# Graph layer on one core: six places for pairs of one-hots instead of four, and the next span's table word loaded inside the loop over pairs

## The chip, the core and the metric

The kernel runs on one NeuronCore of a Trainium2 chip. The metric is the device time of one execution in microseconds (us). TensorE is called PE here and its queue of weight loads PEld, VectorE is DVE, ScalarE is ACT, GpSimd is POOL and SyncE is SP. Each engine has a sequencer that reads the instructions in order, does register work, loads of registers from memory, waits and branches by itself, and hands the rest to its engine.

## What is computed

For 6250 nodes with 256 features and 200,000 edges, sorted by destination (fewer edges the higher the node, since the destinations are drawn as 6250 times a square):

```
agg   = segment_sum(x[src], dst, 6250)
h     = relu(agg @ W_rel + b_rel + x @ W_root)
i, f, g, o = split(h @ W_ih.T + b_ih + b_hh, 4)
h2    = sigmoid(o) * tanh(sigmoid(i) * tanh(g))
out   = layernorm(x + h2 @ W_fc + b_fc)
```

## The kernel before

The nodes lie in 25 groups of 250. The edges lie in chunks of 128, and four chunks are a step (or, in the dense part, a pair of one-hots, which also covers four chunks). The sum over edges is done in two ways.

**Gathered tiles.** For the last 21 groups, as 42 tiles of 125 nodes, POOL gathers the rows of x by the edges' source numbers: per step it copies four columns of source numbers into `idx` (L370) and issues four indirect DMAs (L400) into a ring of seven steps (`rows`). DVE makes a one-hot of the destinations for each step (L906), and PE multiplies it with the gathered rows into `ps_agg` (L476). SP reports each gathered step (L339), and PE's first matmul of a later step gives the ring's slot back to POOL (`steps_summed`, L396). The first seven steps gather from x itself (L385) before the main loop.

**Dense groups.** For the first four groups, where the edges are many, the adjacency is built as a matrix of counts. A window is ten nodes and holds two spans of five nodes; a group has 25 windows and 50 spans. For each span a packed word in `table` (written by DVE in the setup, L856) says which chunks it covers. PE and DVE each walk the same windows, spans and pairs: `unpack` (L297) loads the word into a register (L299) and splits it into first and past (L300), and a loop whose length is known only at run time goes over the span's pairs. In it DVE (`span`, L884) waits for a free place (`pairs_summed`, L891), makes `rel` (L892), `hot_lo` (L894) and `hot_key` (L897), and PE (`windows`, L436) waits for `pairs_ready` (L449), multiplies the four chunks of the pair (L451), and reports the place free. `next_pair` (L305) counts in registers. There are four places (`PAIRS`). Each window begins with a matmul that zeroes its bank (L441) and ends with a marker (L434), after which ACT copies it into `adj` (L639). After a group's 25 windows, `adj` is multiplied with x (L464) in seven batches, loaded into the memory of the pairs' places.

**Order.** Each engine walks a list of turns. A turn has four parts. In a part, PE does half of a tile's steps (`part_sum`, which begins with a load of its own from the table, L484), then a quarter of the gate matmuls of the group before (L537), then the part's windows: three each in the turns of the first dense group (four in its last part), two, two, three and two in those of the other three dense groups, whose last turn has seven windows for the four parts. The windows of one part are called a burst here. After the fourth part come the first layer (L519, L524) and the last (L545). DVE does the same order: one-hots of the part, then the pairs of its burst, then the pieces of the cell and the norm. So there are 8 bursts in the first dense group, around 105 to 362 us, and 12 in each of the others, around 602 to 796, 1000 to 1174 and 1365 to 1540 us.

**Setup.** DVE works out the tables from the destinations, splits x into a high and a low half piece by piece (written to `x_parts`), and reduces the source numbers to what `hot_lo` and `key` need (L858 to L866). POOL starts its first step when the table of tiles is there (L361) and the edges are in (L362).

Of the kernel before, what the change touches and what calls it, by code (L numbers as in the profile page):

```python
# [34 lines left out]
PAIRS = 4  # L35
# [22 lines left out]
T_COLS = T_SPAN + SPANS  # L58
# [67 lines left out]
def gnn_kernel(nc, x, xT, xb, srcT, dstT, dstq, w_rel, w_root, w_ihT, w_fc, b_rel, b_ih, b_hh, b_fc, out):  # L126
# [7 lines left out]
    with ExitStack() as ctx:  # L134
        def sb(name, shape, dt=f32):
            return ctx.enter_context(nc.sbuf_tensor(name, shape, dt))
# [14 lines left out]
        src_sb = sb("src_sb", [P, CHUNK_COLS], i32)  # L151
# [41 lines left out]
        dst_next = flat[0:QP, QPC * CHUNK:(QPC + 1) * CHUNK].bitcast(i32)  # L193
        cell_flat = cell[:, :, :].rearrange("p i n -> p (i n)")
# [47 lines left out]
        edges_in = sem("edges_in")  # L242
        bias_in = sem("bias_in")
# [53 lines left out]
        def unpack(engine, regs, at):  # L297
            packed, first, past = regs
            engine.reg_load(packed, table[0:1, at:at + 1] if isinstance(at, int) else table[0:1, ds(at, 1)])  # L299
            engine.reg_alu(first, packed, PACK, ALU.python_divide)  # L300
            engine.reg_alu(past, first, -PACK, ALU.mult)
            engine.reg_add(past, past, packed)
            return engine.snap(first, min_val=0, max_val=CHUNKS - 1), engine.snap(past, min_val=1, max_val=CHUNKS)
# [9 lines left out]
        @block.sync  # L313
        def _(sp):
            sp.dma_start(dstq_sb, dstq[0:QP * QPC * CHUNK].rearrange("(p c e) -> p c e", p=QP, c=QPC)).then_inc(dstq_in, 16)
            sp.dma_start(dst_next, dstq[QPC * CHUNK:(QP + 1) * QPC * CHUNK].rearrange("(p e) -> p e", p=QP)[:, 0:CHUNK]).then_inc(dstq_in, 16)
            sp.dma_start(src_sb[:, :], srcT).then_inc(edges_in, 16)
            sp.dma_start(dst_i, dstT).then_inc(edges_in, 16)
            sp.sem_inc(gathered, RING)
            for i in SP_PIECES:  # L320
                wait_split(sp, i)
                sp.dma_start(piece_target(i), piece(i)).then_inc(piece_out[i % PARTS], 16)
            for i in range(PARTS + 1):
                sp.wait_ge(piece_out[i], 16 * max(len(range(i, X_WHOLE, PARTS)), 1))
            sp.dma_start(wroot_sb[:, :, :], w_root.rearrange("(k p) n -> p k n", p=P)).then_inc(weights_in, 16)
            sp.dma_start(wrel_sb[:, :, :], w_rel.rearrange("(k p) n -> p k n", p=P)).then_inc(weights_in, 16)
            wih_v = w_ihT.rearrange("(k p) n -> p k n", p=P)
            sp.dma_start(wih_sb[:, :, 0:D_H], wih_v[:, :, 0:D_H]).then_inc(weights_in, 16)
            sp.dma_start(wih_sb[:, :, D_H:3 * D_H], wih_v[:, :, 2 * D_H:4 * D_H]).then_inc(weights_in, 16)
            sp.dma_start(wfc_sb[:, :, :], w_fc.rearrange("(k p) n -> p k n", p=P)).then_inc(weights_in, 16)  # L330

            sp.wait_ge(table_ready, 1)
            steps = sp.value_load(table[0:1, T_STEPS:T_STEPS + 1], min_val=2 * TILES, max_val=MAX_STEPS)
            sp.wait_ge(gathered, 2 * RING)
            with sp.Fori(1, (steps + (RING - 1)) // RING) as r:
                for k in range(RING):
                    for j in range(QC):
                        sp.wait_ge(landed[k][j], r * 16 + 16)
                    sp.sem_inc(gathered, 1)  # L339

        @block.gpsimd
        def _(pool):
# [19 lines left out]
            pool.wait_ge(edges_in, 32)  # L362
# [6 lines left out]
            def copy_index(chunk, k, j):  # L369
                g.tensor_copy(idx[:, k % RING, j:j + 1], src_sb[:, ds(chunk + j, 1)]).then_inc(idx_copied, 1)  # L370
# [5 lines left out]
            for k in range(RING):  # L376
# [6 lines left out]
                pool.sem_inc(steps_begun, 1)  # L383
                for j in range(QC):
# [24 lines left out]
        def _(pe):  # L409
# [18 lines left out]
            pe.reg_mov(place, 0)  # L428
            pe.reg_mov(step_0, 0)
# [6 lines left out]
            def windows(w0, n_windows):  # L436
                for i in range(n_windows):
# [4 lines left out]
                    for side in range(2):  # L442
                        at = w * 2 + (T_SPAN + side)
                        o = bank[:, side * SCOLS:(side + 1) * SCOLS]
                        first, past = unpack(pe, pe_regs, at)
                        with pe.Fori(first, past, QC):
# [5 lines left out]
                            last.then_inc(pairs_summed, 1)  # L452
                            next_pair(pe, pair_0, place, more_places)
# [284 lines left out]
        def _(dve):  # L738
# [101 lines left out]
            dve.sem_inc(table_ready, 1)  # L840
            split_pieces(POOL_PIECES, PARTS)
# [16 lines left out]
            dve.wait_ge(edges_in, 32)  # L858
            v.tensor_copy(dst_u[:, :], dst_i).then_inc(setup, 1)
            v.tensor_scalar(src_part, src_sb[:, :], P - 1, None, ALU.bitwise_and).then_inc(setup, 1)  # L860
            v.tensor_scalar(src_high, src_sb[:, :], P.bit_length() - 1, None, ALU.logical_shift_right).then_inc(setup, 1)
            n_setup[0] += 3
            dve.wait_ge(setup, n_setup[0])
            link(v.tensor_copy(src_lo[:, :], src_part))
# [11 lines left out]
            dve.reg_mov(place, 0)  # L876
            step_0 = dve.alloc_register("step_0")
# [6 lines left out]
            def span(w, side):  # L884
                at = w * 2 + side
                static = isinstance(w, int)
                first, past = unpack(dve, dve_regs, at + T_SPAN)
                with dve.Fori(first, past, QC) as c:
# [6 lines left out]
                                    src_lo[:, ds(c, QC)].rearrange("p (q c) -> p q c", c=2).unsqueeze(2).to_broadcast([P, PQ, P, 2]), ALU.is_equal)  # L895
                    dve.wait_ge(rel_made, s + 1)
# [187 lines left out]
```

## Time and profile before

| | |
|---|---|
| runs of the kernel before | 1822.73, 1830.2, 1832.34 us (median 1830.2) |
| profiled execution, own time | 1824.41 us |
| its span, first to last instruction | 1822.5 us |
| mean granted PE clock | 0.91 of full speed |

The page gives the busy time of each engine and its share of the span; register work, loads into registers, branches and waits are not counted as busy. In the chain of work that ended last, and among the waits, "issue" is time in which the engine waited for nothing that the profile shows, and PEldq, DVEq or POOLq mark the sequencer's own steps, which only the views by line list.

### The profile page before, as it was taken

How to read it: one execution, taken by the hardware profiler on the slowest of the kernel's cores; microseconds unless marked ns; L12 is line 12 of the kernel's file. 1: busy time of each engine (PE TensorE's matmuls, PEld its weight loads, DVE VectorE, ACT ScalarE, POOL GpSimd, SP SyncE). 2: the span in 40 equal slices, each digit the busy share in tenths (PEclk: the TensorE clock that was granted, in tenths of full speed). 3: DMA queues.
4: the chain of work that ended last, by engine and by line, in shares of the span. 5: the costliest groups of instructions: out<-in, count | busy, mean ns of one | idle time of the engine just before them, and what ended most of it. 6: DMA issues, size and time to landing. Idle time of an engine off the chain costs nothing.

```text
span 1822.5 us, 31499 instructions
## 1 busy us (share of the span) xinstructions
PE 1513.5 (83%) x6882; PEld 1213.0 (67%) x6883; DVE 815.9 (45%) x1763; ACT 418.5 (23%) x743; POOL 1281.0 (70%) x1926
## 2 busy tenths in 40 slices
PE   0157688697988898788998889899988888999997
PEld 0023355486767676667887667688876676888886
DVE  8877666431322654531324565422244654222332
ACT  0001021110112332220222333212223332222333
POOL 5875877777777877877777668776763668656640
PEclk9976677698988998889999999999998998999999
DMA  9563555576766555567766445576652455766540
GB/s 342 209 233 87 150 161 145 157 225 207 215 195 180 162 162 165 161 198 223 223 206 180 138 133 166 160 246 217 203 155 77 133 146 161 225 189 177 150 122 18
DMA packets 131966, 319.14 MB, mean 175 GB/s; under 512 B 17295, under 2 KB 68268, under 8 KB 130198
## 3 DMA queue, kind: packets, MB, share of 16 engines
q0 software_dynamic: 75264, 245.95, 46.4%
q10 hardware_dynamic: 52632, 54.80, 9.5%
q1 hardware_dynamic: 3936, 16.62, 2.4%
q8 instruction: 82, 1.34, 0.3%
q14 instruction: 52, 0.43, 0.1%
HBM read 298.10 MB, written 19.20 MB: 174 GB/s over the span
## 4 chain that ended last, share of the span: by engine, by line
PE 48%; POOL 21%; issue 19%; DVE 4%; DMA 3%; DVEq 3%; POOLq 1%; ACT 0%; ACTq 0%; SPq 0%
PE ps_blk L537 20%; POOL rows L400 14%; PE ps_agg L476 9%; PE ps_win L464 6%; POOL idx L370 6%; PE ps_y L545 4%; PE ps_blk L519 3%; PE ps_blk L524 3%; PE ps_tr L451 1%; DMA hot_key<-in_xb 1%; POOL rows L385 1%; PE ps_win L451 1%; DMA rows<-x_parts,idx 1%; POOLq L370 1%; DMA wih_sb<-in_x 1%
## 5 line engine op out<-in xcount | busy, mean ns | idle before, releaser
L400 POOL DMA_INDIRECT rows<-x_parts,idx x924 | 963.5, 1043 | 453.5 <-PE ps_agg L476 157.6
L537 PE MATMUL ps_blk<-cell,wih_sb 128*128 128x250 f32 x2400 | 545.5, 385 | 2.9 <-issue 2.2
L537 PEld LDWEIGHTS ps_blk<-cell,wih_sb 128*128 128x128 f32 x2400 | 464.1, 196 | 69.5 <-issue 8.8
L476 PE MATMUL ps_agg<-rows,onehot 128*125 x1112 | 341.8, 462 | 153.2 <-SPq L339 70.8
L476 PEld LDWEIGHTS ps_agg<-rows,onehot 128*125 128x125 f32 x1112 | 234.1, 216 | 227.5 <-issue 175.9
L906 DVE SCALAR_TENSOR_TENSOR onehot<-iota_f,tile_first,dst_u 128x500 f32 (+1 forms) x278 | 207.0, 746 | 291.7 <-PE ps_agg L476 171.6
L370 POOL COPY idx<-src_sb 128x1 int32 x956 | 264.4, 277 | 16.7 <-issue 9.7
L664 ACT ACTIVATE cell<-ps_blk,bg_sb 128x250 f32<-128x250 f32 x300 | 140.8, 470 | 544.0 <-PE ps_blk L537 470.2
L897 DVE TENSOR_TENSOR hot_key<-iota_h,rel 128x980 f16 x263 | 174.4, 663 | 0.4 <-issue 0.4
L464 PE MATMUL ps_win<-adj,hot_key 128*128 128x250 f32 x784 | 170.7, 375 | 2.4 <-DMA hot_key<-in_xb 1.5
L464 PEld LDWEIGHTS ps_win<-adj,hot_key 128*128 128x128 f32 x784 | 148.0, 190 | 21.6 <-DMA hot_key<-in_xb 4.0
L892 DVE TENSOR_SCALAR rel<-key,span_key x263 | 66.7, 254 | 186.0 <-issue 116.8
L451 PE MATMUL ps_win<-hot_key,hot_lo 128*128 x640 | 113.1, 315 | 34.4 <-issue 20.2
L894 DVE TENSOR_TENSOR hot_lo<-iota_h,src_lo 128x512 f16 x263 | 141.5, 538 | 0.3 <-issue 0.3
L451 PE MATMUL ps_tr<-hot_key,hot_lo 128*128 x412 | 83.2, 312 | 51.3 <-issue 36.3
L451 PEld LDWEIGHTS ps_win<-hot_key,hot_lo 128*128 x640 | 63.7, 100 | 78.2 <-issue 57.5
L519 PE MATMUL ps_blk<-x_t,w_sb 128*128 128x250 f32 x400 | 105.0, 398 | 0.6
L932 DVE TENSOR_TENSOR cell<-cell 128x250 f32<-128x250 f32 x100 | 42.1, 421 | 129.1 <-ACT cell L664 98.1
L451 PEld LDWEIGHTS ps_tr<-hot_key,hot_lo 128*128 x412 | 40.7, 99 | 89.0 <-issue 70.6
L937 DVE TENSOR_TENSOR cell<-cell 128x250 f32<-128x250 f32 x100 | 40.0, 420 | 124.5 <-ACT cell L657 102.8
L524 PE MATMUL ps_blk<-cell,w_sb 128*128 128x250 f32 x400 | 94.6, 378 | 0.0
L639 ACT ACTIVATE adj<-ps_win 128x490 f32<-128x490 f32 x58 | 59.7, 1029 | 146.8 <-PE ps_win L434 90.5
(125 smaller groups left out, 914.2 us busy)
## 6 DMA issues: line engine op xcount, KB each, us to landing
hot_key<-in_xb ACTq DMA_DIRECT2D x28, 896.0 KB
rows<-x_parts,idx POOLq DMA_INDIRECT x924
x_t<-in_xT ACTq DMA_DIRECT2D x25, 250.0 KB
x_n<-in_x ACTq DMA_DIRECT2D x25, 250.0 KB
out<-y ACTq DMA_DIRECT2D x25, 250.0 KB
x_parts<-wih_sb SPq DMA_DIRECT2D x4, 1024.0 KB, 6.8
wih_sb<-in_x ACTq DMA_DIRECT2D x6, 512.0 KB, 9.7
x_parts<-cell SPq DMA_DIRECT2D x2, 1024.0 KB, 7.6
```

The source lines that it names most:

```text
L370: g.tensor_copy(idx[:, k % RING, j:j + 1], src_sb[:, ds(chunk + j, 1)]).then_inc(idx_copied, 1)
L400: g.indirect_dma_start(rows_f[:, k * QC + j, :], None, x_parts, bass.IndirectOffsetOnAxis(ap=idx[:, k, j:j + 1], axis=0)).then_inc(landed[ ...
L451: last = mm(o, hot_lo[:, ds(half, 1), j // 2, :, j % 2].squeeze(1), hot_key[:, ds(half, 1), j // 2, :, j % 2].squeeze(1), start=False, sto ...
L464: last = mm(ps_win[:, c * GN:(c + 1) * GN], xs[:, b, c * P:(c + 1) * P], adj[:, i * X_BATCH + b, :], start=(i == 0 and b == 0 and c == 0), ...
L476: ins = mm(o, onehot[:, hot * QC + j, 0:TN], rows[:, ds(slot + j, 1), :].squeeze(1), start=(first and j == 0), stop=False)
L519: mm(ps_blk[m % BANKS][:, 0:GN], wroot_sb[:, k, m * P:(m + 1) * P], x_t[:, k, :], start=(k == 0), stop=False)
L524: last = mm(ps_blk[m % BANKS][:, 0:GN], wrel_sb[:, k, m * P:(m + 1) * P], agg_t[:, k, :], start=False, stop=(k == KI - 1))
L537: last = mm(o, wih_sb[:, k, col:col + P], h_t[:, k, :], start=(k == 0), stop=(k == KH - 1))
L664: nc.scalar.activation(dst[:, j, :], ps_blk[b % BANKS][:, 0:GN], fn, bias=bg_sb[:, bias + j:bias + j + 1]).then_inc(gate_done, 1)
L894: v.tensor_tensor(hot_lo[:, ds(half, 1), :, :, :].squeeze(1), iota_h[:, 0:P, :].unsqueeze(1).to_broadcast([P, PQ, P, 2]), src_lo[:, ds(c, ...
L897: v.tensor_tensor(hot_key[:, ds(half, 1), :, :, :].squeeze(1), iota_h[:, :, :].unsqueeze(1).to_broadcast([P, PQ, SCOLS, 2]), rel[:, ds(hal ...
L906: v.scalar_tensor_tensor(onehot[:, ds(hot, QC), 0:TN], iota_f[:, 0:TN].unsqueeze(1).to_broadcast([P, QC, TN]), nodes, dst_u[:, ds(c, QC)]. ...
```

## The change

`PAIRS` goes from 4 to 6, so `rel`, `hot_lo` and `hot_key` have six places. The room comes from the source numbers: they stay in memory as 16-bit numbers (`src_u`), are brought in as 32-bit numbers into the last slot of the ring `rows` (`src_i`), and DVE copies them from there right after it has reported the table of tiles; POOL's first step waits for that copy, and its seventh waits until DVE has read the 32-bit numbers. POOL's copies into `idx` read 16-bit numbers. The load of a span's word leaves `unpack` and becomes `load_span`: one before the first window, and one in the body of each loop over pairs, for the span after; on PE it stands behind the four matmuls of the pair, on DVE between `hot_lo` and the wait before `hot_key`. Since it stands in the body, it is done once for each pair.

```diff
-PAIRS = 4
+PAIRS = 6
...
-T_COLS = T_SPAN + SPANS
+T_COLS = T_SPAN + SPANS + 1
...
-        src_sb = sb("src_sb", [P, CHUNK_COLS], i32)
+        src_u = sb("src_u", [P, CHUNK_COLS], u16)
...
+        src_i = flat[:, (RING - 1) * QC * D_ROW:(RING - 1) * QC * D_ROW + CHUNK_COLS].bitcast(i32)
...
+        src_short = sem("src_short")
+        src_read = sem("src_read")
...
-        def unpack(engine, regs, at):
+        def load_span(engine, regs, at):
+            engine.reg_load(regs[0], table[0:1, at:at + 1] if isinstance(at, int) else table[0:1, ds(at, 1)])
+
+        def unpack(engine, regs):
             packed, first, past = regs
-            engine.reg_load(packed, table[0:1, at:at + 1] if isinstance(at, int) else table[0:1, ds(at, 1)])
             engine.reg_alu(first, packed, PACK, ALU.python_divide)
...
-            sp.dma_start(src_sb[:, :], srcT).then_inc(edges_in, 16)
+            sp.dma_start(src_i, srcT).then_inc(edges_in, 16)
...
             pool.wait_ge(table_ready, 1)
-            pool.wait_ge(edges_in, 32)
+            pool.wait_ge(src_short, 1)
...
-                g.tensor_copy(idx[:, k % RING, j:j + 1], src_sb[:, ds(chunk + j, 1)]).then_inc(idx_copied, 1)
+                g.tensor_copy(idx[:, k % RING, j:j + 1], src_u[:, ds(chunk + j, 1)]).then_inc(idx_copied, 1)
...
                 pool.sem_inc(steps_begun, 1)
+                if k == RING - 1:
+                    pool.wait_ge(src_read, 2)
...
             pe.reg_mov(place, 0)
+            load_span(pe, pe_regs, T_SPAN)
...
-                        first, past = unpack(pe, pe_regs, at)
+                        first, past = unpack(pe, pe_regs)
                         with pe.Fori(first, past, QC):
...
                             last.then_inc(pairs_summed, 1)
+                            load_span(pe, pe_regs, at + 1)
                             next_pair(pe, pair_0, place, more_places)
...
             dve.sem_inc(table_ready, 1)
+            dve.wait_ge(edges_in, 32)
+            v.tensor_copy(src_u[:, :], src_i).then_inc(src_short, 1)
             split_pieces(POOL_PIECES, PARTS)
...
-            dve.wait_ge(edges_in, 32)
             v.tensor_copy(dst_u[:, :], dst_i).then_inc(setup, 1)
-            v.tensor_scalar(src_part, src_sb[:, :], P - 1, None, ALU.bitwise_and).then_inc(setup, 1)
-            v.tensor_scalar(src_high, src_sb[:, :], P.bit_length() - 1, None, ALU.logical_shift_right).then_inc(setup, 1)
-            n_setup[0] += 3
+            v.tensor_scalar(src_part, src_i, P - 1, None, ALU.bitwise_and).then_inc(src_read, 1)
+            v.tensor_scalar(src_high, src_i, P.bit_length() - 1, None, ALU.logical_shift_right).then_inc(src_read, 1)
+            n_setup[0] += 1
             dve.wait_ge(setup, n_setup[0])
+            dve.wait_ge(src_read, 2)
...
             dve.reg_mov(place, 0)
+            load_span(dve, dve_regs, T_SPAN)
...
-                first, past = unpack(dve, dve_regs, at + T_SPAN)
+                first, past = unpack(dve, dve_regs)
...
                                     src_lo[:, ds(c, QC)].rearrange("p (q c) -> p q c", c=2).unsqueeze(2).to_broadcast([P, PQ, P, 2]), ALU.is_equal)
+                    load_span(dve, dve_regs, at + (T_SPAN + 1))
                     dve.wait_ge(rel_made, s + 1)
```

## Rows read from the trace of the kernel before

**Rows 1.** The page: busy times of the engines, and the chain's shares.

```profile
PE 1513.5 (83%) x6882; PEld 1213.0 (67%) x6883; DVE 815.9 (45%) x1763; ACT 418.5 (23%) x743; POOL 1281.0 (70%) x1926
...
PE 48%; POOL 21%; issue 19%; DVE 4%; DMA 3%; DVEq 3%; POOLq 1%; ACT 0%; ACTq 0%; SPq 0%
```

**Rows 2.** Busy time by stretch, all engines, then granted clock and DMA.

```profile
105.00:152.50 47.50, 36.55 (x146) 17.93 (x145) 39.41 (x98) 3.07 (x3) 23.46 (x31) 0.62 0.36 109
152.50:865.00 712.50, 583.77 (x2564) 449.80 (x2563) 318.31 (x693) 146.33 (x248) 561.55 (x848) 0.85 0.61 178
865.00:1822.50 957.50, 884.52 (x4159) 741.14 (x4157) 374.87 (x864) 267.84 (x491) 621.79 (x960) 0.96 0.55 163
```

**Rows 3.** Waits of POOL in 100 to 600, 600 to 865, 865 on (total, times, longest).

```profile
POOL rows L400 <- PE ps_agg L476: 19.4, 1, 19.4
...
POOL rows L400 <- PE ps_agg L476: 6.0, 5, 3.0
...
POOL rows L400 <- PE ps_agg L476: 132.2, 18, 24.9
```

**Rows 4.** Waits of PE in 105 to 345, 152.5 to 865, and 865 on (two).

```profile
PE ps_agg L476 <- SPq L339: 18.7, 4, 5.8
...
PE ps_agg L476 <- SPq L339: 69.6, 18, 6.0
...
PE ps_agg L476 <- DVE onehot L906: 9.3, 4, 5.6
...
PE ps_agg L476 <- SPq L339: 1.2, 1, 1.2
```

**Rows 5.** Timeline of PE at the end of a late burst of four pairs.

```profile
1441.80 0.68 PE L451 MATMUL ps_tr<-hot_key,hot_lo 128*128 x4
1443.54 0.74 PE L451 MATMUL ps_tr<-hot_key,hot_lo 128*128 x4 [1.06 <-issue]
...
1445.64 1.67 PE L476 MATMUL ps_agg<-rows,onehot 128*125 x6 [1.10 <-issue]
```

**Rows 6.** PE's sequencer at L299, whole run (ns: shortest, median, longest).

```profile
L299 PEldq TENSOR_LOAD <-table x200: 296/302/323, 108.6 to 1537.9; - x100
L299 PEldq FUSED_REGOPS  x150: 51/53/79, 598.9 to 1537.8; - x150
```

**Rows 7.** The chain around the first span on DVE.

```profile
105.35 0.31 DVEq L299
...
105.69 0.23 DVEq L300
```

**Rows 8.** The chain inside the first burst.

```profile
134.41 0.20 issue
134.61 1.00 PE ps_tr L451 x4
135.61 0.69 issue
```

**Rows 9.** Pairs of the run; of the first burst; its span loads; L451 by stretch.

```profile
L897 DVE TENSOR_TENSOR hot_key<-iota_h,rel 128x980 f16 x263 | 174.4, 663 | 0.4 <-issue 0.4
...
L897 DVE TENSOR_TENSOR hot_key<-iota_h,rel x31: 655/662/670, 106.8 to 145.5; 128x980 f16 x31
...
L299 PEldq TENSOR_LOAD <-table x6: 297/309/322, 108.6 to 145.1; - x6
...
865.00:1300.00 435.00, 32.13 (x200) 19.44 (x200) 0.97 0.63 187
```

**Rows 10.** Timeline of DVE and of PE around one pair of the third burst.

```profile
189.19 0.66 DVE L897 TENSOR_TENSOR hot_key<-iota_h,rel 128x980 f16 x1
...
190.09 0.74 PE L451 MATMUL ps_win<-hot_key,hot_lo 128*128 x4 [0.51 <-DVE hot_key L897]
```

**Rows 11.** Groups by line: POOL's copy of source numbers; a 32-bit to 16-bit cast.

```profile
L370 POOL COPY idx<-src_sb x956: 192/193/1197, 32.0 to 1769.5; 128x1 int32 x192
...
L859 DVE CAST dst_u<-hot_key 128x1568 uint16<-128x1568 int32 x1 | 1.0, 976 | 0.2 <-DVE table L856 0.2
```

## The prediction

> **What bounds the kernel now.** The page says first that no engine is full: PE is busy 83% of the span and POOL 70%, and PE holds 48% of the chain, POOL 21% and "issue" 19% [rows 1]. Such shares are averages over stages, so I cut the span where the waits change their direction [rows 2].
>
> POOL's waits give the cuts [rows 3]. POOL waits once for PE, 19.4 us, until 152.4 us, while PE works through the first burst. From there to 865 us it waits 6.0 us in all, the longest 2.98 us at 657 us: it runs freely, and PE waits for gathered steps 18 times, 69.6 us [rows 4]. From 865 us on POOL waits 132.2 us for PE, and PE waits 1.2 us for steps. So PE sets the pace up to 152 us, POOL from 152 to 865 us, and PE after that. PE's time in the middle stretch is worth nothing except where it is late enough to hold POOL up.
>
> Inside the bursts, what limits PE? Not its array: the four matmuls of the last pair of a late burst begin 1.74 us after those of the pair before and take 0.74 us, with 1.06 us idle put down to issue [rows 5]. In the first burst an idle of 0.20 us stands between pairs of one span and one of 0.69 us where a span ends [rows 8]. This is PE's sequencer: branch, counters, load of the word, unpacking. And not DVE: in the tightest place that I found (third burst) the one-hot is done at 189.19 + 0.66 = 189.85 us and PE's matmul starts at 190.09 [rows 10]; in the late groups they are several us ahead. That idle is labelled with hot_key only because hot_key came last; what ended it was the sequencer. So DVE's places don't hold PE, although DVE waits for them.
>
> **The change, part by part.**
>
> *Two more places.* They remove waits of DVE for PE. PE doesn't wait for pairs, so nothing is gained there; what follows on DVE (next one-hots, cell products) comes earlier. From 865 us on PE's waits for one-hots of tiles are 9.3 us in four places, the longest 5.6 us [rows 4]; that one stands behind a group's product, where DVE waits for PE first, and the shorter ones are about as long as PE's own start of a part (1.10 us of issue, [rows 5]). I take 0; the bound is a gain of 9.3 us.
>
> *The load on PE.* A load takes 0.302 us on PE's sequencer, and the register work for a changing address 0.053 us [rows 6]. On DVE the load (0.31 us) and the next step stand 0.34 us apart [rows 7]. I take 0.35 us for a load on PE, and 0.45 us with the address work and its gap. The bounds are 0.05 us (the sequencer goes on while the load is under way, only its issue is paid) and 0.49 us (the whole extra idle of a span's end, 0.69 - 0.20, which holds the unpacking too, [rows 8]). Nothing covers it: it stands behind the pair's last matmul, when PE has nothing queued.
>
> Where the loop runs once for a span, the load only moves from behind the branch to ahead of it. Two things are added. The body's loads count pairs, not spans: 263 pairs [rows 9] for 200 spans, all 63 extra ones in the first dense group, since a late group has 200 / 4 = 50 pairs for its 50 spans [rows 9]. And the load for a burst's first span, which PE's sequencer did under the queued gate matmuls, now stands at the end of the burst before, with the load of `part_sum` or the first layer queued behind it.
>
> - First burst: 31 pairs, 6 loads before [rows 9]. Of the 31 loads after, 5 are those between spans; 26 are new on PE's path: 26 x 0.35 = 9.1 us. POOL waits for exactly this (19.4 us), so it starts its free stretch 9.1 us later. Bounds 1.3 and 12.7 us.
> - The seven other bursts of this group: 82 pairs for 44 spans, 38 + 7 = 45 loads, 15.8 us. PE waits 18.7 us for steps in 105 to 345 us [rows 4], which absorbs it almost; the last burst lies behind most of these waits, so I add 1.0 us. Bounds 0 and 3.
> - Second dense group: 12 bursts. Four of them lie ahead of POOL's wait at 657 us: 4 x 0.45 = 1.8 us. The other eight are absorbed by waits for steps. Bounds 0.4 and 2.4.
> - Last two dense groups, where PE sets the pace: 24 bursts x 0.45 = 10.8 us. Bounds 24 x 0.1 = 2.4 and 24 x 0.59 = 14.2.
>
> *The load on DVE.* It stands under `hot_lo` and takes 0.34 us [rows 7] of its sequencer, 25 more times in the first burst. There DVE's pairs follow one another at (145.5 - 106.8) / 30 = 1.29 us on the mean [rows 9], span ends included and partly held back by PE; with the loads that becomes at most 1.29 + 25 x 0.34 / 30 = 1.57 us. PE's mean pace becomes 1.20 + 5 x 0.49 / 30 + 25 x 0.35 / 30 = 1.57 us [rows 8] as well, so DVE barely stays off the path: 0, with an upper bound of 1 us.
>
> *Setup.* POOL's first step now waits for a cast of 128x1568 numbers on DVE; a cast of this size takes 0.976 us [rows 11]. POOL's first steps lie on the chain of waits. 1.0 us, bounds 0 and 1.5. The piece splits that DVE does next are 1.0 us later too. The seventh step's wait for `src_read` is for two operations that DVE does right after the table of spans, while POOL has six steps to issue first: 0.
>
> *16-bit source numbers on POOL.* 956 copies of 0.193 us [rows 11], in series with the indirect DMAs. The trace has no POOL copy that changes the type; DVE's cast of 1568 columns runs at the usual pace, and on POOL one column is all fixed cost. I take 0. In the stretch that POOL sets there are 848 / 2 = 424 copies [rows 2]; 0.05 us more on each (a quarter) would be 21 us, my upper bound. A cheaper copy would be worth at most the same the other way; I see no reason for one, as only 128 numbers are read either way.
>
> The sum is 1.0 + 9.1 + 1.0 + 1.8 + 10.8 = 23.7 us. The profiled execution took 1824.4 us, so it would take 1848.1. The median shown is 5.8 us above it and the three runs spread over 9.6 us, so a median may lie at 1848 to 1854; I forecast 1851.
>
> A rule bears on the load. The Trainium skill, Perfetto Trace Analysis, section on sequencer-only instructions, says that a sequencer reads its next instruction only after it has executed one and pushed its semaphore update. It speaks against this change: by it a load behind the matmuls is paid in full, as in my sum; were it wrong, the first rival below would hold. The trace agrees as far as it goes, with 0.34 us from a load of 0.31 us to the next step [rows 7], but there the next step needs the word.
>
> **Rivals.**
>
> 1. *Faster: the load runs beside what follows it.* Each load in the trace is followed by a step that needs its word, so its 0.30 us may be latency that `next_pair` and the branch would now cover. From the third pair of a late burst on, the loads are on the path: (50 - 24) x 2 = 52 spans x 0.30 = 15.6 us gained, against 24 x 0.1 at the bursts' ends, and -1.5 + 1.3 in the first burst, and the setup's 1.0: -12.4 + about 0 in the middle, so 1812 us by the profiled execution, 1815 as a median. It decides as soon as more than two thirds of a load are covered. Against it: every step of a sequencer in the chain follows the one before by its length and a small gap.
> 2. *The load costs, but less, and the sum stays in the noise.* At 0.10 to 0.15 us a load the terms shrink to about 3.5 + 1 + 5 us with the setup's 1.0 inside: +4 to +9 us, 1831 to 1836.
> 3. *The places pay some back.* If the 9.3 us of waits for one-hots [rows 4] were due to DVE's waits for places, the sum would be 14 us: 1842.
> 4. *POOL's copy costs more.* With 0.05 us on each, 21 us come on top: 1872.
> 5. *The change doesn't reach what it aims at* is my forecast in part: six places are filled, yet PE's pace in a burst doesn't move.
>
> **Chances.** About 9 us (0.5%) is what a measurement of this kernel can tell from no change. Forecast 0.62; rival 1 0.13; rival 2 0.11; rival 3 0.06; rival 4 0.08. So faster 0.13, same 0.12, slower 0.75. The likeliest case alone spans 1838 to 1864 (bounds of its terms, and the median's 6 us). The whole range leaves out rival 1 and the far ends: 1833 to 1876.
>
> **What would show it.** PE's steps in the first burst 1.55 us apart inside a span instead of 1.20, the burst about 9 us longer, and POOL's wait before 152 us grown to about 28 us. In a late burst the same 1.74 us between the last two pairs, and 1.10 us before the next part's first matmul grown to about 1.55. 263 loads on each sequencer. DVE's waits for places shorter, without effect. If instead the 1.74 us shrink to about 1.45, rival 1 holds; if POOL's copies are longer than 0.193 us, rival 4. What else would make it wrong: a granted PE clock in the late stretch that falls from its 0.96 [rows 2], because PE pauses more often between matmuls; 0.01 less over 884 us of busy time is up to 9 us.

## The result, and the profile after

The changed kernel takes 1838.65 us (median of 7 runs, 1836.6 to 1843.2); the kernel before 1830.2 (7 runs beside them, 1822.73 to 1832.34). The ratio is 1.0058, with a 95% interval of 1.0038 to 1.0078: a small loss (+8.45 us in the medians), of the sign that was predicted and about half its size or less (the forecast was +20.8 us). The profiled execution took 1836.6 us against 1824.4.

The page of the changed kernel: the engines' busy times, then the shares of the chain [rows 1].

```profile
PE 1508.9 (82%) x6882; PEld 1211.9 (66%) x6883; DVE 834.1 (45%) x1764; ACT 418.1 (23%) x743; POOL 1269.0 (69%) x1926
...
PE 49%; POOL 19%; issue 18%; DVEq 5%; DVE 5%; DMA 4%; POOLq 1%; ACT 0%; ACTq 0%; SPq 0%
```

PE and POOL do no more work. DVE is busy for 18 us more with operations of the same length (`hot_lo` 0.539 us in the mean against 0.538): its loads stand between them now, so they overlap less. The kernels with one engine's load below bear that out: with DVE's load alone DVE is busy for 832.0 us, with PE's alone for 815.2. DVE's waits for a free place got shorter, as forecast, and nothing came of it (before, then after: total, times, longest):

```profile
DVE rel L892 <- PE ps_win L451: 62.6, 19, 17.4
```

```profile
DVE rel L904 <- PE ps_win L459: 24.6, 19, 6.4
```

The three stretches of [rows 2], with their borders moved by what the first burst grew:

```profile
105.00:162.10 57.10, 37.41 (x147) 17.94 (x146) 42.38 (x98) 3.07 (x3) 22.28 (x31) 0.60 0.32 100
162.10:875.00 712.90, 580.86 (x2562) 446.99 (x2561) 326.21 (x693) 146.13 (x248) 561.43 (x851) 0.85 0.62 179
875.00:1834.70 959.70, 881.81 (x4160) 742.70 (x4158) 381.49 (x864) 267.59 (x491) 611.91 (x958) 0.96 0.56 162
```

The first stretch is 9.6 us longer for the same instructions, the middle one as long as before, the last one 2.2 us longer. POOL's waits for PE in 100 to 600, in 600 to 875 and from 875 us on (total, times, longest) answer to [rows 3], and PE's waits for gathered steps in 105 to 345 and in 152.5 to 865 us to [rows 4].

```profile
POOL rows L407 <- PE ps_agg L485: 30.6, 2, 30.5
...
POOL rows L407 <- PE ps_agg L485: 8.4, 5, 5.4
...
POOL rows L407 <- PE ps_agg L485: 147.1, 21, 25.4
```

```profile
PE ps_agg L485 <- SPq L344: 5.2, 1, 5.2
...
PE ps_agg L485 <- SPq L344: 52.3, 15, 7.0
```

POOL's first wait grew from 19.4 to 30.5 us, and PE's waits for steps in the first dense group shrank from 18.7 to 5.2: what PE lost there was taken out of them. The loads, by sequencer:

```profile
L301 PEldq TENSOR_LOAD <-table x264: 297/302/488, 57.5 to 1552.9; - x132
L301 DVEq TENSOR_LOAD <-table x264: 299/306/1866, 73.9 to 1541.6; - x132
```

That is one ahead of the first window and one for each of 263 pairs, against 200 [rows 6]. PE in the first burst:

```profile
129.73 1.00 PE L459 MATMUL ps_win<-hot_key,hot_lo 128*128 x4 [0.59 <-issue]
131.33 1.00 PE L459 MATMUL ps_win<-hot_key,hot_lo 128*128 x4 [0.60 <-DVE hot_key L910]
132.88 1.00 PE L459 MATMUL ps_win<-hot_key,hot_lo 128*128 x4 [0.56 <-DVE hot_key L910]
```

Pairs of one span follow one another at 1.55 to 1.60 us, where they did at 1.20 [rows 8]. From its zeroing matmul to PE's next `ps_agg` matmul the burst takes 50.63 us against 40.96, so +9.67. Now the late burst of [rows 5], first its start and its marker in the kernel before, which [rows 5] leave out, then the changed kernel, where it lies 16.7 us later:

```profile
1440.67 0.27 PE L441 MATMUL ps_win<-zero_bf 128*128 128x245 bf16 x1
...
1444.37 0.17 PE L434 MATMUL ps_tr<-zero_bf 128*128 128x1 bf16 x1
```

```profile
1457.34 0.27 PE L449 MATMUL ps_win<-zero_bf 128*128 128x245 bf16 x1
...
1458.46 0.60 PE L459 MATMUL ps_tr<-hot_key,hot_lo 128*128 x4
1459.77 0.74 PE L459 MATMUL ps_tr<-hot_key,hot_lo 128*128 x4 [0.70 <-issue]
1461.13 0.17 PE L442 MATMUL ps_tr<-zero_bf 128*128 128x1 bf16 x1 [0.61 <-issue]
1462.37 1.42 PE L485 MATMUL ps_agg<-rows,onehot 128*125 x5 [1.07 <-issue]
```

This isn't what I forecast. The last two pairs stand 1.31 us apart instead of 1.74; the marker comes 1.36 us behind the last pair instead of 0.83; and the next part begins 1.24 us behind the marker, as before (1.27). From the burst's first matmul to the next part it is 5.03 us against 4.97. The last pair comes earlier by one load, and what follows it later by one, so the burst as a whole gained almost nothing and lost almost nothing.

### The profile page after: what moved, and what is told of

Its sections match the earlier page's. It is cut to its first block, busy times and chain, and to the rows that moved or that the text cites. A ratio compares the mean times of both kernels' runs of the same rounds, so it can differ in the third digit from the quotient of the medians.

```text
span 1834.7 us, 31625 instructions
## 1 busy us (share of the span) xinstructions
PE 1508.9 (82%) x6882; PEld 1211.9 (66%) x6883; DVE 834.1 (45%) x1764; ACT 418.1 (23%) x743; POOL 1269.0 (69%) x1926
## 3 DMA queue, kind: packets, MB, share of 16 engines
q8 instruction: 83, 1.36, 0.3%
## 4 chain that ended last, share of the span: by engine, by line
PE 49%; POOL 19%; issue 18%; DVEq 5%; DVE 5%; DMA 4%; POOLq 1%; ACT 0%; ACTq 0%; SPq 0%
PE ps_blk L546 19%; POOL rows L407 12%; PE ps_agg L485 9%; PE ps_win L473 6%; POOL idx L375 5%; PE ps_y L554 4%; PE ps_blk L528 4%; PE ps_blk L533 3%; DMA rows<-x_parts,idx 2%; PE ps_win L459 2%; POOL rows L392 1%; PE ps_tr L459 1%; DVE hot_key L910 1%; DVEq L301 1%; DMA hot_key<-in_xb 1%
## 5 line engine op out<-in xcount | busy, mean ns | idle before, releaser
L407 POOL DMA_INDIRECT rows<-x_parts,idx x924 | 951.5, 1030 | 480.4 <-PE ps_agg L485 186.2
L375 POOL CAST idx<-src_u 128x1 int32 x956 | 272.8, 286 | 13.5 <-issue 10.8
L473 PE MATMUL ps_win<-adj,hot_key 128*128 128x250 f32 x784 | 170.4, 374 | 1.2 <-DMA hot_key<-in_xb 1.2
L473 PEld LDWEIGHTS ps_win<-adj,hot_key 128*128 128x128 f32 x784 | 148.3, 190 | 19.3 <-DMA hot_key<-in_xb 2.7
L459 PE MATMUL ps_tr<-hot_key,hot_lo 128*128 x412 | 79.1, 308 | 45.8 <-issue 32.5
```

Source lines behind the costliest of these rows:

```text
L375: g.tensor_copy(idx[:, k % RING, j:j + 1], src_u[:, ds(chunk + j, 1)]).then_inc(idx_copied, 1)
L407: g.indirect_dma_start(rows_f[:, k * QC + j, :], None, x_parts, bass.IndirectOffsetOnAxis(ap=idx[:, k, j:j + 1], axis=0)).then_inc(landed[ ...
L459: last = mm(o, hot_lo[:, ds(half, 1), j // 2, :, j % 2].squeeze(1), hot_key[:, ds(half, 1), j // 2, :, j % 2].squeeze(1), start=False, sto ...
L473: last = mm(ps_win[:, c * GN:(c + 1) * GN], xs[:, b, c * P:(c + 1) * P], adj[:, i * X_BATCH + b, :], start=(i == 0 and b == 0 and c == 0), ...
```

## The experiments

All of them are edits of the kernel before or of the changed one. The kernel before ran beside each group of them, with medians of 1827.2, 1827.35 and 1826.85 us; ratios are to those. The two columns for bursts are differences to the kernel before in the profiled execution: each burst is taken from its zeroing matmul to PE's next matmul of another kind in the timeline. The 24 late bursts are those of the last two dense groups, and sum to 119.3 us before.

| kernel | median us | ratio, 95% interval | first burst | 24 late bursts | profiled run, us |
|---|---|---|---|---|---|
| the change | 1838.65 | 1.0058 (1.0038 to 1.0078) | +9.67 | +1.4 | 1836.6 |
| places and 16-bit numbers only | 1827.13 | 1.0001 (0.9982 to 1.0021) | +0.01 | +0.1 | 1820.64 |
| both loads only, four places | 1846.62 | 1.0107 (1.0086 to 1.0127) | +9.24 | +1.3 | 1837.92 |
| the same again | 1847.57 | 1.0095 (1.0062 to 1.0127) | +9.22 | +1.4 | 1847.52 |
| PE's load only | 1838.52 | 1.0061 (1.0039 to 1.0084) | +10.64 | +2.0 | 1838.52 |
| DVE's load only | 1830.01 | 0.9999 (0.9985 to 1.0014) | +3.31 | -1.1 | 1827.11 |
| change, PE's load behind the loop | 1834.75 | 1.0039 (1.0023 to 1.0055) | +3.22 | +0.4 | 1836.62 |
| kept load ahead of each burst | 1841.6 | 1.0067 (1.0045 to 1.0089) | +0.64 | +13.0 | 1844.92 |
| kept load behind each burst | 1855.75 | 1.0154 (1.0133 to 1.0176) | +1.45 | +17.1 | 1855.22 |
| pair counts for PE | 1807.56 | 0.9899 (0.9876 to 0.9921) | +0.16 | -7.5 | 1806.02 |
| the same with five places | 1811.31 | 0.9917 (0.9889 to 0.9944) | +0.50 | -6.9 | 1801.26 |

### Places and loads apart

Places only: the changed kernel, with the load back in `unpack`. Loads only: the kernel before, with `load_span` on both engines as in the change.

```diff
 # places only, against the changed kernel (on PE and on DVE; the loads ahead of the loops go too)
-        def unpack(engine, regs):
+        def unpack(engine, regs, at):
             packed, first, past = regs
+            load_span(engine, regs, at)
...
-                            load_span(pe, pe_regs, at + 1)
...
 # loads only, against the kernel before (the same on DVE, between hot_lo and the wait)
-                        first, past = unpack(pe, pe_regs, at)
+                        first, past = unpack(pe, pe_regs)
...
+                            load_span(pe, pe_regs, at + 1)
```

> The changed kernel with the loads put back into the unpacking, once per span: six places, 16-bit source numbers, the setup as changed. Theory A: within 3 us of the kernel before, since PE never waits for a pair; first burst within 0.5 us of before. Rival B: +5 us or more. Rival C (the places pay something back that the loads hide): 4 to 9 us faster than before.

> The kernel before with only the loads moved into the loops over pairs (four places, 32-bit source numbers). Theory A (the 63 added loads on PE's sequencer in the first dense group are the cost, and the move by itself costs nothing because PE's lead over a burst is fixed where its last gate matmul is queued): the whole slowdown is here, +8 to +12 us against the kernel before; first burst 9.5 us longer, each late burst of four or six pairs within 0.1 us of before. Rival B (places, source numbers or the setup carry part of it): under +5 us here.

The places, the 16-bit numbers and the setup's cast are worth nothing together: 1.0001. The loads alone carry the loss. But loads alone lost 1.07%, more than the change with its 0.58%, so I ran them again.

> The kernel before with both loads in the loop, four places, 32-bit numbers, again. The earlier run gave a ratio of 1.0107, more than the whole change (1.0058). If that stands (1.009 or more again), six places or the 16-bit numbers pay back some 0.4% of the loads' price; if it falls to 1.004 to 1.008, the difference was the scatter between programs' executions and the places pay nothing here either.

It stayed, with 1.0095, so the payback that this expectation names isn't excluded. The 14 runs lie apart, four at 1835.2 to 1838.4 us and ten at 1845.6 to 1852.9; all 7 of the change lie at 1836.6 to 1843.2. The two profiles of the loads caught one of each kind. PE stands within 3 us of the same place in both up to the last dense group, and there they part. This is that group, from the start of its first burst to the start of its last, in the first of them and in the second, as in [rows 2]; both hold the same 700 matmuls:

```profile
1382.90:1550.40 167.50, 141.45 (x700) 112.25 (x699) 97.04 (x217) 53.77 (x87) 102.41 (x147) 0.94 0.45 126
```

```profile
1384.80:1559.00 174.20, 149.33 (x700) 118.86 (x699) 96.93 (x217) 53.76 (x87) 105.69 (x151) 0.88 0.44 124
```

The same matmuls keep PE busy for 7.9 us more where the granted clock is 0.88 instead of 0.94, and the stretch is 6.7 us longer; that is most of the 9.6 us between the two executions. The granted clock is a mean of the clock's two levels, 1.2 and 2.4 GHz. It differs as much between executions of the same work elsewhere. Here are the last two dense groups by execution, each from its first burst's start to its last burst's start, with 712 or 713 matmuls in the third group and 700 or 701 in the fourth. The two rows "same work" are kernels that came out the same as the kernel before (see below).

| execution | third group: us, PE busy, clock | fourth group: us, PE busy, clock |
|---|---|---|
| kernel before | 169.2, 145.9, 0.95 | 170.4, 146.7, 0.91 |
| same work | 171.6, 148.9, 0.92 | 170.4, 146.7, 0.91 |
| same work | 173.6, 151.0, 0.90 | 171.3, 148.6, 0.90 |
| the change | 173.5, 149.7, 0.90 | 167.5, 141.4, 0.94 |
| both loads, first profile | 173.5, 149.8, 0.90 | 167.5, 141.5, 0.94 |
| both loads, second profile | 172.9, 148.8, 0.91 | 174.2, 149.3, 0.88 |
| kept load ahead of each burst | 180.0, 153.3, 0.89 | 178.9, 152.3, 0.88 |
| kept load behind each burst | 184.5, 153.6, 0.88 | 184.3, 154.4, 0.86 |

So the two profiles differ by the granted clock in one stretch, not by the work. The profiled execution of the loads alone that had the higher clock (1837.9 us) is as long as that of the whole change (1836.6 us), and has the same bursts. Why ten of 14 executions of the loads alone are longer and none of the 7 of the change isn't shown by anything that I ran; that six places or the 16-bit numbers pay something back when both loads are in the loops stays possible.

### One engine's load at a time

```diff
-                        first, past = unpack(pe, pe_regs, at)
+                        first, past = unpack(pe, pe_regs)
...
                             last.then_inc(pairs_summed, 1)
+                            load_span(pe, pe_regs, at + 1)
```

> The kernel before with only PE's load in the loop over pairs; DVE loads once per span as before. Theory A: as with both loads, +8 to +12 us, first burst 9 to 10 us longer. Rival G (DVE's longer sequencer work in the loop paces the first burst): +3 us or less.

> The kernel before with only DVE's load in the loop over pairs. Theory A: within 3 us of before, since DVE's pace with the load (about 1.5 us a pair in the first burst) lies near PE's 1.2 us and a pair's places give it a lead of four; if its pace sets the first burst after all, that one grows by up to 25 x 0.2 = 5 us (rival G: as with both loads, +8 to +12 us).

PE's load alone gives the change's whole loss, 1.0061. DVE's alone gives nothing that can be told from the scatter (0.9999), though its first burst is 3.3 us longer. In the changed kernel the chain through the first burst shows DVE's loads on it:

```profile
125.81 0.30 DVEq L301
...
127.23 0.30 DVEq L301
...
128.64 0.31 DVEq L301
```

A pair takes DVE 1.42 us there. With PE at 1.20 us a pair that is too slow, which fits the 3.3 us; with PE at 1.55 it is hidden.

### PE's load once for a span

The changed kernel, with PE's load moved out of the pair loop's body to right behind it; DVE's load stays in the body.

```diff
                             last.then_inc(pairs_summed, 1)
-                            load_span(pe, pe_regs, at + 1)
                             next_pair(pe, pair_0, place, more_places)
+                        load_span(pe, pe_regs, at + 1)
```

> The changed kernel with PE's load of the next word behind the loop over pairs instead of in its body, so once per span (200 instead of 263); DVE's load stays in the body. Theory A: within 3 us of the kernel before, first burst within 1 us of before, late bursts as in the changed kernel. Rival D (where the load stands costs, not how often): +8 us or more, as the changed kernel. If DVE's loads pace the first burst, it stays 5 us or more longer than before.

PE does 201 loads and the first burst's growth falls from 9.7 to 3.2 us, which is what DVE's load alone gave (3.3). The seven others of the group fall from +13.3 to +0.9 us. The ratio falls by a third of the loss only, to 1.0039, so theory A missed here: +7.5 us in the medians instead of 3 at most. Its profiled execution lost 5 us at one other place, where a group's product waited 5.5 us, until 1206 us, for its batch of x, while none of these waits was over 0.6 us before; I don't know whether its other runs do so too. With DVE's load alone at 0.9999 and places alone at 1.0001 the sum of the parts would be less than 1.0039; that gap stays open.

### Does a load at a burst's start cost what one at its end costs?

This is the step that was wrong. I took it that PE's sequencer does the first span's load under the queued gate matmuls for nothing. The rival: the sequencer hands over the last gate matmul at a fixed lead before the burst begins, and all that it does from there on sets the end of the burst, wherever in it that stands. First, two kernels with a load into a register that nothing reads:

```diff
             def windows(w0, n_windows):
+                pe.reg_load(unused, table[0:1, T_SPAN:T_SPAN + 1])   # or behind the loop over windows
                 for i in range(n_windows):
```

> The kernel before with one more load of a table word on PE, its value unused, ahead of each burst (44 loads). Theory A (the lead of PE's sequencer is fixed at the last queued gate matmul): it costs 0.36 us in each late burst although gate matmuls are still running when it executes, 24 x 0.36 = 9 us in the late stretch plus up to 1.5 us earlier. Rival E (covered by the queued gate matmuls, as the prediction took it): within 2 us of before, and each late burst within 0.1 us.

> The kernel before with the same unused load behind each burst's marker. Both theories: 0.36 us before the next part's first matmul in the bursts that a part's sum follows; with the first layer behind the burst the same 0.36 us. 24 x 0.36 = 9 us in the late stretch plus up to 1.5 us. It is the yardstick for the run with the load at the start.

These tell nothing of the load, since it isn't executed. In the first one's trace, PE's sequencer has only the 200 loads of `unpack`:

```profile
L299 PEldq TENSOR_LOAD <-table x200: 296/302/325, 109.2 to 1537.9; - x100
```

They are the kernel before twice more, at 1827.45 us (1.0006, 0.9988 to 1.0024) and 1829.47 us (1.0014, 0.9994 to 1.0034), and show what scatter a kernel with the same work has. So I took a load whose value is kept and bounded:

```diff
             def windows(w0, n_windows):
+                pe.value_load(table[0:1, T_STEPS:T_STEPS + 1], min_val=2 * TILES, max_val=MAX_STEPS)   # or behind the loop
                 for i in range(n_windows):
```

> The kernel before, with one more load into a register that is kept (with its bound check, some 0.66 us of PE's sequencer, worked out from 0.36 us for a load and its gap and 0.3 us for the check) ahead of each burst's first window, under the queued gate matmuls. 44 bursts, 24 of them in the last two dense groups. Theory A (the sequencer hands over the last gate matmul at a fixed lead before the burst, so all that it does after that sets the burst's end): each late burst ends about 0.66 us later, 24 x 0.66 = 16 us, some 2 us more from the first burst and the setup's end, so about +15 us, 1842. Theory E (what the sequencer does under queued gate matmuls is covered, as the prediction had it): within 2 us of the kernel before, 1828.

> The same kept load, behind each burst's last window instead of ahead of its first. Theory A: the same as ahead of the burst, about +15 us, 1842, within 3 us of the run with the load at the start. Theory E: +16 us here, where the start costs nothing, so the two differ by over 12 us.

From its start to the sequencer's next step the kept load takes 0.68 us in the median, at either place (0.32 + 0.16 + 0.02 us and the gaps between them). Ahead of the burst it costs 0.54 us in each of the 24 late bursts on the mean, behind it 0.71 us. So a load under the queued gate matmuls isn't free. The same late burst, with the load at its start and then at its end:

```profile
1457.24 0.27 PE L442 MATMUL ps_win<-zero_bf 128*128 128x245 bf16 x1
...
1458.86 0.75 PE L452 MATMUL ps_tr<-hot_key,hot_lo 128*128 x4 [0.34 <-issue]
1460.65 0.74 PE L452 MATMUL ps_tr<-hot_key,hot_lo 128*128 x4 [1.04 <-DVE hot_key L898]
...
1462.90 2.06 PE L477 MATMUL ps_agg<-rows,onehot 128*125 x4 [1.06 <-issue]
```

```profile
1464.92 0.27 PE L441 MATMUL ps_win<-zero_bf 128*128 128x245 bf16 x1
...
1468.60 0.17 PE L434 MATMUL ps_tr<-zero_bf 128*128 128x1 bf16 x1
1470.94 1.64 PE L477 MATMUL ps_agg<-rows,onehot 128*125 x3 [2.17 <-issue]
```

With the load at the start, 1460.65 - 1457.24 = 3.41 us pass to the last pair, against 1443.54 - 1440.67 = 2.87 before; at the end, 2.34 us pass from the marker to the next part against 1.27 (1.07 more in this burst; 0.64 to 0.73 more in 16 of the 24). And this is the lead: PE's sequencer around this burst, in the kernel before (the wait's arithmetic for the burst's first window, then its loads), in the changed one (the same arithmetic, then its unpacking) and in the one with the kept load at the start (that load, then the loads of `unpack`).

```profile
L440 PEldq ALU_OP  x1: 32/32/32, 1436.9 to 1436.9; - x1
...
L299 PEldq TENSOR_LOAD <-table x4: 296/301/313, 1437.2 to 1442.7; - x4
```

```profile
L448 PEldq ALU_OP  x1: 32/32/32, 1453.6 to 1453.6; - x1
...
L305 PEldq FUSED_REGOPS  x4: 177/183/183, 1453.8 to 1459.3; - x4
```

```profile
L437 PEldq TENSOR_LOAD <-table x1: 317/317/317, 1453.5 to 1453.5; - x1
...
L299 PEldq TENSOR_LOAD <-table x4: 302/306/307, 1454.4 to 1459.8; - x4
```

The sequencer's first step of the burst stands 3.8 us ahead of the burst's first matmul (1440.67 - 1436.9, 1457.34 - 1453.6, 1457.24 - 1453.5), whether that step is a piece of arithmetic (before and after) or the kept load. With the kept load it is 3.78 or 3.79 us in 33 of the 36 bursts of the last three dense groups, and 4.2 to 4.6 in the other three. The sequencer has that much in hand and no more. A span takes it some 1.8 us (four loads from 1437.2 to 1442.7), so the lead is used up in the first two pairs: with the kept load the third pair already waits 0.34 us, and without it the fourth is the first to wait. A step more there makes the last pairs later by most of its length.

The time of the whole kernel didn't come out as either theory has it. The load at the start costs +14.8 us in the medians, as theory A says (+15) and against theory E (within 2). The load at the end costs +28.9 us, where both had 15 or 16, so that the two differ by 14 us and not by 3 at most. In the profiled executions the last two dense groups, by the table above, are 19.3 and 29.2 us longer than before. Of this the bursts in them give 11.9 and 15.8, and 7.4 and 13.4 us lie between the bursts, where the work is the same. The same matmuls keep PE busy for 13.0 and 15.4 us more in the two groups, at granted clocks of 0.89 and 0.88, and of 0.88 and 0.86. So most of what the bursts don't explain goes with a lower clock. Why the clock was lower in these two isn't shown.

### Less for PE's sequencer

The kernel before, with the number of pairs of each span in the table beside the packed word. PE loads the count and loops from 0, so that the unpacking goes (0.24 us a span from its start to the next step).

```diff
-                        first, past = unpack(pe, pe_regs, at)
-                        with pe.Fori(first, past, QC):
+                        pe.reg_load(pe_regs[0], table[0:1, ds(at, 1)])      # at is in the counts' part
+                        with pe.Fori(0, pe.snap(pe_regs[0], min_val=1, max_val=STEPS)):
...
+            link(v.tensor_copy(table[:, T_COUNT:T_COUNT + SPANS], row_i[:, 0:SPANS]))
```

> The kernel before with a second table row that holds the number of pairs of each span, which the setup has anyway: PE loads that and loops over it, and does no unpacking (0.24 us from its start to the next step). Theory A (the bursts' length is PE's sequencer work from the last gate matmul on): each late burst of four spans 4 x 0.24 = 0.96 us shorter, 24 late bursts with 100 spans 24 us, first burst 1.4 us: 20 to 26 us faster. Rival E (the first two pairs of a late burst are covered by the queue, as the prediction had it): 52 spans x 0.24 = 12.5 us, 11 to 15 us faster. Rival F (PE then waits for DVE's one-hots or something else): under 8 us.

> Pair counts in the table for PE and the load once per span, as in the earlier run of 1807.6 us, and besides five places instead of four and the 16-bit source numbers. Theory A: places pay nothing, so within 0.3% of 1807.6 us, ratio to the kernel before 0.987 to 0.993. Rival: once PE is quicker in the bursts, DVE is the one that is late, and the places pay: 5 us or more faster still, a ratio of 0.987 or less.

This is the fastest: 1807.56 us, 1.0% below the kernel before and 19.7 us in the medians, nearly what theory A forecast. But the bursts don't say so. The 24 late bursts are 7.5 us shorter, where theory A had 24, and the first isn't shorter at all (+0.16), where it had 1.4. The trace shows why the forecast of the bursts was too high: two register moves now stand where the unpacking stood,

```profile
L447 PEldq MOVE  x400: 29/35/43, 107.9 to 1519.1; - x134
```

and from the first of them to the next step it takes 0.18 us, so 0.06 us a span are saved and not 0.24. For the 100 spans of the late bursts that is 6.0 us, and 3.1 for the 52 spans that rival E counts; the measured 7.5 is nearer to theory A's way of counting. The same late burst has 1.65 us between its last two pairs, against 1.74:

```profile
1426.03 0.62 PE L452 MATMUL ps_tr<-hot_key,hot_lo 128*128 x4
1427.68 0.74 PE L452 MATMUL ps_tr<-hot_key,hot_lo 128*128 x4 [1.02 <-issue]
```

The profiled execution ends 18.3 us earlier. PE is 1.7 us ahead at the first burst, 6.1 at the first burst of the third dense group, 13.1 at that of the fourth and 18.9 at the last burst. The waits of the first part after a product are 3.5 and 3.1 us instead of 5.6 and 5.5, and the granted clock from 865 us on is 0.97 instead of 0.96 [rows 2]. I can't tie these to the missing steps: so the gain is measured, and less than half of it is explained. Five places instead of four add nothing: 1.0% and 0.8% below, with intervals that overlap. So I see no gain from a place more even when PE's sequencer is a little quicker.

## Why the prediction was right, and where its size was off

- **What bounds PE in the bursts: right.** More places alone change nothing (1.0001); a load more on PE's sequencer costs (1.0061), and 0.06 us less of it a span makes the late bursts 7.5 us shorter.
- **The first burst: right.** 9.1 us forecast, 9.67 measured, 0.37 us for each of the 26 extra loads. POOL's wait was to grow to about 28 us, it grew to 30.5. The whole shift of PE was 9.6 us at 158 us and between 9 and 10.2 at all twelve bursts of the second group: POOL, which sets the pace there, carried it to 865 us unchanged.
- **The other bursts of the first group: right.** 15.8 us of loads forecast, 13.3 us measured, absorbed by waits for steps (18.7 to 5.2 us). The 1.0 us that the sum has for them didn't show: PE's shift is 9.6 us behind the first burst and 9.6 at the first burst of the second group.
- **The late bursts: wrong, and with them half of the sum.** The step was that "the load for a burst's first span, which PE's sequencer did under the queued gate matmuls, now stands at the end of the burst before": 24 x 0.45 = 10.8 us, and 1.8 us in the second group. Measured: 1.4 us in 24 bursts and 0.5 in 12. The load does stand at the end now, and costs there about what I said (last pair to marker 0.83 to 1.36, where I had looked for it behind the marker, which stayed at 1.27 and 1.24). But it had cost nearly the same at the start, where a lead of 3.8 us only postponed the bill to the last pairs. The move is a wash. My error was to call a step free because the engine behind it was busy; what counts is whether the sequencer's lead lasts to the burst's end, and in a burst of four pairs it doesn't. [Rows 5] had the sign of it: the last pair waits for issue. So had the prediction itself, whose rival 1 says that from the third pair on the loads are on the path; then the first load isn't free either. The Trainium skill, Perfetto Trace Analysis, Tensor Engine instruction, says that a matmul is pushed into a wait queue, after which the sequencer is free for the next instruction. By that it can be ahead; the trace agrees, and gives the size, 3.8 us.
- **DVE's load: right in the change, wrong alone.** Forecast 0 with at most 1 us, because PE's pace would be 1.57 us too. It holds in the change, where the first burst grows no more than with PE's load alone (9.67 and 10.64 us); alone the same load costs the first burst 3.3 us.
- **Setup: 1.0 us too much. POOL's copies: right in effect.** The first burst begins at 109.50 us against 109.75, so the 1.0 us didn't reach it. A copy into `idx` is a cast now, 0.205 us in the median against 0.193 [rows 11]. That is the sign that I gave for rival 4, but 0.012 us on 424 copies are 5 us and not 21, and even they don't show where POOL sets the pace (PE's shift is 9.6 us at 158 us and 9.2 at 793), nor with the places alone (1.0001). So rival 4 falls.

```profile
L375 POOL CAST idx<-src_u x956: 194/205/3552, 32.8 to 1780.9; 128x1 int32 x192
```

The rivals, and the sum:

- **Rival 1** (the load runs beside what follows) falls: the 63 extra loads on PE are paid in full, (9.67 + 13.29) / 63 = 0.36 us. The sign that I gave for it misleads: the 1.74 us between the last two pairs did shrink, to 1.31, but only because the load of the first span left the lead, and the time came back behind the last pair. The Trainium skill, Perfetto Trace Analysis, sequencer-only instruction, says that the sequencer fetches the next instruction only when it has executed one and pushed its semaphore update. The trace agrees, here also where the next step needs nothing of the load. **Rival 2** (a load costs 0.10 to 0.15 us, +4 to +9 us in all) has the right size for the median, +8.45 us, and the wrong cause: a load costs 0.36 us, and there are fewer of them to pay for. **Rival 3** (places pay back) falls for the places alone; with both loads in the loops it stays open, since the loads without the places lost 1.07 and 0.95% and the change 0.58%. Against it stands that PE's load alone, with four places, lost no more than the change (0.61%).
- **The sum again.** 23.7 us were forecast, and 12.2 us came between the profiled executions. 9.67 us from the first burst and 1.4 us from the late ones make 11; the two terms of 1.0 us didn't come, nor did more than 0.5 of the 1.8 and 1.4 of the 10.8 us. So 1851 us was 12 us too high, and 1838.65 lies at the lowest edge of the likeliest case (1838 to 1864). That 11 and 12.2 agree is partly luck: in between, PE's shift goes from 9.2 us at 793 to 13.1 at 1001 us (a wait for a gathered step at 863 us of 7.6 us, and one after the first product of 7.4 us instead of 5.6), to 17.4 at the end of the third group and 16.9 at 1505 us, and back to 12 at the end. The table of the two last groups accounts for the later part: the third group is 4.3 us longer at a clock of 0.90 instead of 0.95, the fourth 2.9 us shorter at 0.94 instead of 0.91. Both kernels with the same work as the kernel before drift likewise, by 3 and 5 us at 1131 us.

## What to carry to other kernels

A sequencer that runs ahead of its engine has a lead of so many microseconds, and it is a stock that each register step draws on. Here it was 3.8 us, two pairs' worth: moving a step within a burst that used it up changed nothing, and only fewer steps did. Before moving a load, count how often it runs at the new place: once for each pair instead of once for each span made nearly all of PE's loss in the first burst here. And look at what sets the pace of the loop (here the consumer's sequencer) before giving the loop more buffers.

## What the hardware showed that I hadn't expected

- PE's sequencer stands 3.78 us ahead of its engine behind a run of gate matmuls, the same to 0.01 us in 33 of 36 bursts with the kept load, and in the burst shown also without it.
- The granted clock of a stretch of 170 us differs between executions of the same work: 0.95, 0.92 and 0.90 in the third dense group (169.2, 171.6 and 173.6 us), 0.94 and 0.88 in the fourth with both loads (167.5 and 174.2 us). With a loss of 0.6% under study this is as large as the effect, and only the lengths of the bursts in the timeline told them apart. The two kernels with the kept loads had less in both groups (0.89 and 0.88, 0.88 and 0.86); whether because they pause PE more isn't shown.
